# Own instruction orders for the last batch of a transformer layer: seven idle products out, two fc1 fills and all of fc2 behind the last values

## The reference, cut to what matters

```python
x = x + 0.5 * ffn(layernorm(x))          # called pre below
x = x + attn(layernorm(x))               # its output has a LayerNorm of its own, with gamma and beta
x = x + 0.5 * ffn(layernorm(x))          # called post below

def attn(u):                             # u: 8 batches x 512 tokens x 128, 16 heads of 8
    q, k, v = split(u @ w_qkv)
    w = relu(q @ k.T / sqrt(8))          # for each head 512 x 512
    w = w / (sum(w, -1) + 1e-6)
    y = u + (w @ v) @ w_out + b_out
    return layernorm(y) * gamma + beta

def ffn(r):                              # r: 512 tokens x 128 for each batch
    h = layernorm(r) * ln_gamma + ln_beta
    z = silu(h @ dequant(fc1) + fc1_bias) @ dequant(fc2) + fc2_bias   # 128 -> 512 -> 128
    return r + 0.5 * z
```

## Time and profile before

| | us |
|---|---|
| median of 3 runs | 376.51 (375.6 to 376.83) |
| the profiled execution | 376.51 |
| its span, first to last instruction | 374.7 |
| around the span | 1.8 |
| PE, DVE, ACT, POOL busy | 365.4, 289.7, 230.3, 218.4 |
| mean granted TensorE clock | 1.000 of full |

### The profile page before, as it was taken

How to read it: one execution, slowest core, us unless ns; L and a number is a source line. 1 busy time by engine, 2 the same in 40 slices (tenths; PEclk the granted TensorE clock), 3 DMA queues, 4 the chain that set the end, 5 groups by cost and what they waited for, 6 DMA issues and landing times.

```text
span 374.7 us, 11851 instructions
## 1 busy us (share of the span) xinstructions
PE 365.4 (98%) x4574; PEld 188.8 (50%) x4574; DVE 289.7 (77%) x694; ACT 230.3 (61%) x422; POOL 218.4 (58%) x449
## 2 busy tenths in 40 slices
PE   8899999899999999999999999999999999999997
PEld 7854433344464345453554445653464444533486
DVE  6776778897778978797878978788776876777584
ACT  3377466557847577466847486566856578486503
POOL 7595156448963589337972589438891567146041
DMA  6016006300442016300361006400270005400001
GB/s 209 4 31 170 3 0 162 94 3 2 108 119 59 3 27 148 111 2 3 73 157 58 2 0 156 107 25 2 45 180 33 3 0 128 129 1 3 2 2 59
DMA packets 14103, 22.66 MB, mean 60 GB/s; under 512 B 2528, under 2 KB 3808, under 8 KB 14048
## 3 DMA queue, kind: packets, MB, share of 16 engines
q1 hardware_dynamic: 11456, 17.83, 19.5%
q10 hardware_dynamic: 2592, 4.07, 3.3%
HBM read 3.54 MB, written 2.10 MB: 15 GB/s over the span
## 4 chain that ended last, share of the span: by engine, by line
PE 85%; DVE 6%; POOL 3%; issue 2%; DMA 2%; ACT 1%; SPq 0%; POOLq 0%; DVEq 0%; ACTq 0%
PE o_bank L607 30%; PE scores L584 16%; PE post_bank L536 9%; PE pre_bank L536 9%; PE pre_bank L541 4%; PE pre_bank L542 2%; PE post_bank L541 2%; DVE probs L1192 2%; PE post_bank L542 2%; PE post_bank L559 2%; PE pre_bank L559 2%; PE pre_bank L529 2%; PE o_bank L517 1%; PE post_bank L529 1%; PE pre_bank L623 1%
## 5 line engine op out<-in xcount | busy, mean ns | idle before, releaser
L1192 DVE TENSOR_SCALAR probs<-scores 128x512 f32<-128x512 f32 x250 | 160.3, 681 | 47.6 <-PE scores L584 45.9
L896 ACT ACTIVATE probs<-scores 128x512 f32<-128x512 f32 x262 | 141.4, 596 | 60.3 <-PE scores L584 60.2
L607 PE MATMUL o_bank<-probs,v_op 128*32 128x512 f32 x1024 | 135.8, 603 | 0.0
L584 PE MATMUL scores<-q_op,k_op 32*128 32x512 f32 x512 | 75.2, 494 | 0.5
L584 PEld LDWEIGHTS scores<-q_op,k_op 32*128 32x128 f32 x512 | 30.7, 181 | 79.5 <-issue 56.1
L788 ACT ACTIVATE pre_y<-pre_bank,b_sum,col_consts 128x512 f32<-128x512 f32 x28 | 21.8, 779 | 29.4 <-PE pre_bank L559 29.3
L607 PEld LDWEIGHTS o_bank<-probs,v_op 128*32 128x32 f32 x1024 | 21.5, 108 | 29.1 <-issue 25.3
L536 PE MATMUL pre_bank<-w,pre_y 128*32 128x128 f32 x960 | 30.8, 274 | 0.0
L536 PEld LDWEIGHTS pre_bank<-w,pre_y 128*32 128x32 f32 x960 | 25.7, 110 | 8.1 <-issue 7.6
L536 PE MATMUL post_bank<-w,post_y 128*32 128x128 f32 x960 | 29.5, 273 | 0.0
L536 PEld LDWEIGHTS post_bank<-w,post_y 128*32 128x32 f32 x960 | 26.1, 110 | 6.0 <-issue 5.7
(11 more groups left out here) (212 smaller groups left out, 557.2 us busy)
## 6 DMA issues: line engine op xcount, KB each, us to landing
k_op<-k_parts SPq DMA_DIRECT2D x62, 128.0 KB, 2.7
q_op<-q_parts SPq DMA_DIRECT2D x62, 128.0 KB, 2.7
out_dram<-o_rows ACTq DMA_DIRECT2D x7, 256.0 KB, 2.0
pre_x<-in_x_dram ACTq DMA_DIRECT2D x6, 256.0 KB, 2.8
w_int<-in_L_ffn_fc_q_dram SPq DMA_DIRECT2D x2, 256.0 KB, 4.1
rows<-in_lines_dram ACTq DMA_DIRECT2D x1, 256.0 KB, 5.0
s_rows<-in_L_ffn_fc_scales_dram SPq DMA_DIRECT2D x1, 256.0 KB, 6.7
wqk<-in_w_qk_dram SPq DMA_DIRECT2D x1, 256.0 KB, 6.8
```

What stands on the lines that cost most here:

```text
L584: mm(scores[i][:, j, :], k_op[rows, g, P * kt:P * (kt + 1)], q_op[rows, g, :], start=True, stop=True).then_inc(scores_done[i], 1)
L607: last = mm(o_bank[pair][VW * j:VW * (j + 1), :], v_op[:, kt, heads_of(g).start + 2 * j, :], probs[:, s % 2, j, :], start=(odd == 0 and kt ...
L896: activation(probs[:, s % 2, 2 * i + j, :], scores[i][:, j, :], ACT.Relu).then_inc(probs_done[i][j], 1)
L1192: v.tensor_scalar(probs[:, s % 2, 2 * i + j, :], scores[i][:, j, :], 0.0, None, ALU.max).then_inc(probs_done[i][j], 1)
```

## The change

The last batch gets lists of its own: `of_batch` picks `PE_START` and its like for batch 0, `PE_END`, `ACT_END`, `DVE_END` for batch 7 and the common lists otherwise. POOL's list stays. The seven idle products in the steps of the last batch are gone, with `keep_warm`. Fills 2 and 3 of fc1 of the seventh batch leave the steps and stand behind the last values, ahead of `last.op`; all of its fc2 stands behind `last.op`; the idle products there are 13 and not 23. ACT takes three banks in steps 0 to 4 and 8 to 11 (nine steps, before six: 0, 1, 2, 5, 6, 14). The tasks of the seventh batch shift to later steps: on DVE `oT.1` 0 as before, but its `den.1` 1 (was 0), `y_stats` 4 (was 2), `x2` 8 (5), `x2_stats` 9 (6), `hT` 13 (10), `oT.0` 11 and `den.0` 14 (both 12), `a.0` 15 (14); on ACT `store` 5 (2), `y_apply` 6 (4), `hT` 13 (9); on PE `hT` 13 (9), fc1 fills 0 and 1 14 and 15 (11 and 12).

```diff
-BARE_STEPS = (3, 4, 5, 6, 7, 8, 10)
-
-THREE_BY_ACT = (0, 1, 2, 5, 6, 14)
+THREE_BY_ACT = (0, 1, 2, 3, 4, 8, 9, 10, 11)
+
+PE_END = [
+    (["post.fc2.0@-2", "post.fc2.1@-2"], []),
...
+    ([], ["post.fc1.1@-1"]),
+]
 PE_LAST = ([], [
-    "post.fc2.0@-2", "post.fc2.1@-2", "post.fc2.2@-2", "last.op.0@-1", "last.op.1@-1", "post.fc2.3@-2", "warm_up.23@-1",
+    "post.fc1.2@-2", "post.fc1.3@-2", "last.op.0@-1", "last.op.1@-1", "post.fc2.0@-2", "post.fc2.1@-2",
+    "post.fc2.2@-2", "post.fc2.3@-2", "warm_up.13@-1",
...
 ACT_LAST = [
-    "last.hT.0@-1", "last.hT.1@-1", "last.fc1.0.1@-1", "post.store@-2", "last.fc1.1.1@-1", "last.fc1.2.1@-1",
+    "post.fc1.2@-2", "post.fc1.3@-2", "last.hT.0@-1", "last.hT.1@-1", "last.fc1.0.1@-1", "post.store@-2", "last.fc1.1.1@-1", "last.fc1.2.1@-1",
...
+def of_batch(b, start, order, end):
+
+    return start if b == 0 else end if b == B - 1 else order
...
-                for s, (early, late) in enumerate(PE_ORDER if b > 0 else PE_START):
+                for s, (early, late) in enumerate(of_batch(b, PE_START, PE_ORDER, PE_END)):
                     step_scores(b, s)
-                    if b == B - 1 and s in BARE_STEPS:
-                        keep_warm(1)
                     work(b, early)
```

More of the change, by code:

```diff
@@ L88 @@
 ]
-BARE_STEPS = (3, 4, 5, 6, 7, 8, 10)
-THREE_BY_ACT = (0, 1, 2, 5, 6, 14)
+THREE_BY_ACT = (0, 1, 2, 3, 4, 8, 9, 10, 11)
+PE_END = [
+    (["post.fc2.0@-2", "post.fc2.1@-2"], []),
+    (["post.fc2.2@-2", "post.fc2.3@-2"], []),
+    ([], ["post.op@-1"]),
+    ([], []),
+    ([], []),
+    ([], []),
+    ([], []),
+    ([], []),
+    ([], []),
+    ([], []),
+    ([], []),
+    ([], []),
+    ([], []),
+    (["post.hT@-1"], []),
+    ([], ["post.fc1.0@-1"]),
+    ([], ["post.fc1.1@-1"]),
+]
 PE_LAST = ([], [
-    "post.fc2.0@-2", "post.fc2.1@-2", "post.fc2.2@-2", "last.op.0@-1", "last.op.1@-1", "post.fc2.3@-2", "warm_up.23@-1",
+    "post.fc1.2@-2", "post.fc1.3@-2", "last.op.0@-1", "last.op.1@-1", "post.fc2.0@-2", "post.fc2.1@-2",
+    "post.fc2.2@-2", "post.fc2.3@-2", "warm_up.13@-1",
     "last.hT.0@-1", "last.fc1.0.0@-1", "last.fc1.1.0@-1", "last.fc1.2.0@-1", "last.hT.1@-1", "last.fc1.3.0@-1",
@@ L141 @@
 ]
+ACT_END = [
+    [],
+    [],
+    [],
+    [],
+    [],
+    ["post.store@-2"],
+    ["post.y_apply@-1"],
+    [],
+    [],
+    [],
+    [],
+    [],
+    [],
+    ["post.hT@-1"],
+    ["post.fc1.0@-1"],
+    ["post.fc1.1@-1"],
+]
 ACT_LAST = [
-    "last.hT.0@-1", "last.hT.1@-1", "last.fc1.0.1@-1", "post.store@-2", "last.fc1.1.1@-1", "last.fc1.2.1@-1",
+    "post.fc1.2@-2", "post.fc1.3@-2", "last.hT.0@-1", "last.hT.1@-1", "last.fc1.0.1@-1", "post.store@-2", "last.fc1.1.1@-1", "last.fc1.2.1@-1",
     "last.fc1.3.1@-1", "last.store.0@-1", "last.store.1@-1"
@@ L187 @@
 ]
+DVE_END = [
+    ["oT.1@-1"],
+    ["den.1@-1", "a.1@-1", "post.out@-2", "aT@-1"],
+    ["post.y@-1"],
+    [],
+    ["post.y_stats@-1"],
+    [],
+    [],
+    [],
+    ["post.x2@-1"],
+    ["post.x2_stats@-1"],
+    [],
+    ["oT.0"],
+    [],
+    ["post.hT@-1"],
+    ["den.0"],
+    ["a.0"],
+]
 DVE_LAST = [
@@ L517, in warm_up @@
                     mm(o_bank[1][:, 0:P], ident[:, :], ident[:, :], start=True, stop=True)
[L519 to L523, removed]
             def transposes(st, b, rows, done):
@@ L890, in _ @@
             for b in range(B):
-                for s, beside in enumerate(ACT_ORDER if b > 0 else ACT_START):
+                for s, beside in enumerate(of_batch(b, ACT_START, ACT_ORDER, ACT_END)):
                     if STEPS * b + s - 1 > 0:
@@ L1186, in _ @@
             for b in range(B):
-                for s, beside in enumerate(DVE_ORDER if b > 0 else DVE_START):
+                for s, beside in enumerate(of_batch(b, DVE_START, DVE_ORDER, DVE_END)):
                     if STEPS * b + s - 1 > 0:
```

## The result

The changed kernel takes 374.01 us (median of 4 runs, 372.92 to 374.3), the one before 376.66 beside it (4 runs): a ratio of 0.9931, interval 0.9914 to 0.9947, so 2.65 us faster; forecast were 2.7, and 373.8. The profiled execution is one of 374.3 us with a span of 372.5.

A forecast was written before the change was run, and what follows sets the result against it. PE's own list was taken to bound the kernel nearly everywhere, with scores waiting for relus. Savings 2.5 + 0.3 + 0 - 0.2 = 2.6, 2.7 with half of steps 0 to 2's favourable bound: 373.8 us, range 372.0 to 376.0.

The forecast's parts named there:

- Length of a step: Mean length of last-batch steps: bare 1.70 us by two, 1.82 by three; 2.02 with transposes, 2.32 with an fc1 fill.
- steps under 1.5: Sign in the profile after that the forecast is wrong: last-batch steps shorter than 1.5 us.
- So an idle product of 0.42 us costs only 0.21 us of time ... Removing it will return half its price.: Last batch's steps: half of each idle product lies under relus that are late anyway, so removing it returns 0.21 us.
- Both checks: Trace checks of step lengths: steps 7 and 8 with an idle product, mean 1.91; first batch's bare steps 1.81 and 1.74.
- Steps 3 to 12: Last batch, all ten steps bare: 17.7 us plus 0.7 for tasks, 18.4 against 20.87, 2.5 us less.
- Step 13: Last batch: transposes in place of a fill, 2.02 us against 2.32, 0.3 less.
- The rule of the mean: Scores held in one step leave the next less wait, so over several steps the length settles at the two's mean.
- Steps 0 to 2: Start of the last batch, same products, fc2 half a step earlier: change 0, bounds -0.3 and +0.3.
- the last steps: Steps 14 and 15 to the end of the last values: 5.63 us against 5.64, no change.
- the projection and its margin of 0.05 us: Behind the last values: `op` starts where it did, at worst 0.15 later; rival of a late second fill 375.0, chance 0.10.
- Behind the projection: fc2 and idple products behind `op` take 0.3 us more, delaying the last transposes: 0.2 lost, bounds 0 and 0.3.
- the second rival: The clock falls in bare steps 3 to 12: 1.0 us per step, 379.8 if six of ten; chance 0.08.

The follow-up runs named there:

- without idle products alone: The kernel before with only the seven idle products of the last batch's steps taken out, orders unchanged: 376.18 us against 376.73, ratio 0.998.
- fill 1 late: The changed kernel with fill 1 of fc1 behind the last values too, fill 3 behind the projection, 8 idle products there, not 13: 373.66 us, ratio 0.9917 to the kernel before.
- eleven idle products: The changed kernel with 11 idle products behind fc2 at the end and not 13: 373.9 us, ratio 0.9924 to the kernel before.
- no idle products at the end: The changed kernel without the 13 idle products behind fc2 at the end: 375.25 us, 1.2 more than the changed kernel.

## Why the prediction was right, and where not

- **Length of a step.** Right as a mean: by three 1.87 for 1.82 over six steps, by two 1.70 for 1.70 over four, and 2.32 with a fill. Single steps lie between 1.43 and 2.22, and the sign of being wrong "steps under 1.5" was badly chosen.
- **"So an idle product of 0.42 us costs only 0.21 us of time ... Removing it will return half its price."** Wrong for the part alone: 0.08 (run without idle products alone). The prediction set the length of a step by PE and by relus that follow the scores at a fixed distance, and priced other tasks of DVE and ACT apart; where such a task comes first, that engine sets the length. Both checks hid this. In step 7 of the kernel before, DVE was in its statistics until just before its relus fell due at 334.37, and had been at work since 332.59 without a gap: the idle product of the step before had made the room for them, and in the run without idle products these relus are late. In the first batch DVE is full as well (2.00 of 2.00 us), and the check counted steps 7 and 8 and left out step 9, as bare as they are, which lasts 2.36 (46.07 to 48.43): four relus stand there behind the same kind of statistics.

```profile
334.08 0.38 DVE L966 BATCH_NORM_AGGREGATE norm_x_mv<-norm_x_stats 128x2 f32<-128x6 f32 x4
...
45.71 2.60 DVE L1192 TENSOR_SCALAR probs<-scores 128x512 f32<-128x512 f32 x4
48.43 0.50 PE L584 MATMUL scores<-q_op,k_op 32*128 32x512 f32 x4
```

- **Why the sum came out even so.** It was added up from lengths of bare steps and not from the prices of what went, and with the new order and steps by three these lengths hold; there an idle product is worth 0.17.
- **Steps 3 to 12.** 18.0 us, forecast 18.4 from 17.7 and 0.7 for tasks; the tasks cost 0.3. The whole stretch got 2.85 us shorter too, and by the runs that is 0.6 for idle products in the old order, 1.36 for the fills that left, 0.2 for the order of the tasks and 0.67 for the steps by three, which the prediction had lumped into lengths.
- **Step 13.** Forecast 2.02, measured 2.45: its scores still waited 0.93 (held over from step 12) and the transposes of 0.59 came on top. The rule of the mean holds over several steps, not for the one where a task begins.
- **Steps 0 to 2**, the last steps, the projection and its margin of 0.05 us: right within 0.2.
- **Behind the projection.** +0.3 for a forecast of 0.2: two idle products fewer take it back in the profile.
- **The total.** 2.65 for 2.7 is closer than its terms deserve: steps 3 to 12 gave 0.35 more than forecast, step 13 0.4 less, and these cancel by luck.
- **The clock.** It stayed at 1.00, though PE waits 3.7 us in steps 3 to 12 (18.0 less ten times 1.43); the second rival fell. Every such wait was under 0.9 us. The swing of the clock that the Trainium skill tells of (page "TensorE: Matmul & The Clock Gate", section "A second HAM failure mode: psum-queue depth-cycling") did not come there. The runs with fewer idle products behind fc2 show that the risk was real in another place: 2.56 us idle, and the clock at half behind it.

## What to carry to other kernels

Where two engines hand banks back and forth, work out the length of a step from both loops before pricing a task: as long as the relus are what is late, a task beside such a step costs half its time; where other tasks keep the other engine full, it costs almost nothing to leave in and gives nothing when taken out; and what goes beyond the wait costs its whole time. A check of such a price has to cover every step of its kind, also the one that doesn't fit. Move the tasks of the engine that is full to the steps in which it has less to do, and spread those of the waiting engine one to a step; here this was worth more than the idle products. Idle products are cheap where they fill a wait of the engine: first look how long that wait is, and test the clock without them.

## What the runs showed of the hardware that was not expected

The times of most versions fall in two groups some 1.2 us apart (the kernel before: 375.2 to 375.6 and 376.4 to 377.2) with the clock at 1.00 in both. Two profiles, of fill 1 late (372.63 us) and of eleven idle products (373.88 us), agree to 0.1 us up to 60 us, run the same instructions up to the last batch, and differ by 1.2 us from 71 us on: in the second batch the scores of step 2 start at 69.70 in one and at 70.92 in the other. The first, then the second:

```profile
65.44 0.41 DVE L1041 TENSOR_TENSOR a_t<-o_t,rec 128x256 f32<-128x256 f32 x1
65.63 1.36 POOL L1338 TENSOR_TENSOR pre_xr<-pre_xr,b_quarter 128x512 f32<-128x512 f32 x1
69.70 0.51 PE L637 MATMUL scores<-q_op,k_op 32*128 32x512 f32 x4
```

```profile
65.57 1.28 POOL L1338 TENSOR_TENSOR pre_xr<-pre_xr,b_quarter 128x512 f32<-128x512 f32 x1
65.69 1.44 DVE L1041 TENSOR_TENSOR a_t<-o_t,rec 128x256 f32<-128x256 f32 x1
70.92 0.50 PE L637 MATMUL scores<-q_op,k_op 32*128 32x512 f32 x4
```

Two instructions with two inputs each meet here, one on DVE and one on POOL, and the order of their starts decides. Where DVE's starts first it takes 0.41 us. Where POOL's has started, DVE's ends only 0.3 us behind the end of POOL's; it is then 1.03 to 1.48 us long, and PE waits for `aT`. All thirteen profiles of this case agree: the first order stands in the three short ones (fill 1 late, without idle products alone, no idle products at the end), the second in the ten others. A copy to `k_op` that SP issued at 58.8 took 1.63 us in the first profile and 2.14 in the second, and is not what separates the groups: over the thirteen it took 1.63 to 1.88 us in the three short ones and 1.56 to 2.49 in the others. In five of the thirteen the two starts lie less than 0.15 us apart. No run here moves one of them, so that the order is the cause of the two groups rests on this agreement.
